# A fused residual layer on one core: loads reordered at the start, scale factors in the index row, low-rank products in fp32r parts

## The reference, cut to what matters

```
w = weights[cond]                       # (32, 64, 64), one of 200 matrices per sample
x = x + einsum('bct,bcd->bdt', x, w)    # layer 0: mixes the 64 channels
H = einsum('btd,od->bto', x, W)         # layer 1: W is 512 x 512
xa = einsum('btd,brd->btr', x, A[idx])  # rank 16, one of 8 adapters per sample
x = x + H + einsum('btr,bor->bto', xa, Bm[idx]) * scalings[idx]
```

## Time and profile before

| | |
|---|---|
| median of 3 runs | 83.15 us |
| profiled execution | 83.01 us |
| its span | 81.3 us |
| PE (matmul) busy | 74.2 us, 91% |
| DVE busy | 51.6 us, 63% |
| ACT busy | 47.6 us, 59% |
| POOL busy | 35.7 us, 44% |
| DMA | 14.58 MB, mean 179 GB/s |

### The profile page before, as it was taken

The page is one execution under the profiler, slowest core; times in us unless marked ns, Lnnn a source line. Parts: engine busy times, 40 slices in busy tenths (PEclk is TensorE's granted clock), DMA queues, the critical chain, the costliest instruction groups (busy, mean ns, idle before and its releaser), DMA issues.

```text
span 81.3 us, 1928 instructions
## 1 busy us (share of the span) xinstructions
PE 74.2 (91%) x482; PEld 67.8 (83%) x482; DVE 51.6 (63%) x125; ACT 47.6 (59%) x105; POOL 35.7 (44%) x76
## 2 busy tenths in 40 slices
PE   4999299999498999999999999999999999999950
PEld 4975288975396999999999999999999999999940
DVE  3830689150797958684868486948694878548730
ACT  0730696431988929292939394848575757375540
POOL 4200068999847653554455454465355523000000
PEclk9999999999999999999999999999999999999999
DMA  0899655589999879777897879668815452303015
GB/s 0 238 356 225 237 156 108 143 214 194 175 194 224 221 213 235 256 268 189 266 247 220 149 241 250 227 128 265 219 61 130 146 172 79 129 0 129 8 58 204
DMA packets 13198, 14.58 MB, mean 179 GB/s; under 512 B 6786, under 2 KB 8066, under 8 KB 13186
## 3 DMA queue, kind: packets, MB, share of 16 engines
q1 hardware_dynamic: 7714, 9.32, 37.5%
q0 software_dynamic: 4640, 4.23, 25.3%
q10 hardware_dynamic: 832, 0.91, 4.0%
HBM read 10.23 MB, written 4.19 MB: 177 GB/s over the span
## 4 chain that ended last, share of the span: by engine, by line
PE 65%; DMA 16%; DVE 5%; issue 5%; ACT 3%; POOL 2%; POOLq 0%; ACTq 0%
PE z_ps L566 45%; DMA scale_sb<-scales 8%; DMA b_raw<-b_t 8%; PE out_ps L601 4%; PE out_ps L619 4%; PE v_ps L595 4%; PE out_ps L615 4%; PE out_ps L614 4%; ACT w_raw L304 1%; ACT b_high L332 1%; DVE moving L438 1%; DVE b_stack L465 1%; DVE a_table L502 1%; POOL w_sb L248 1%; ACT moving L295 1%
## 5 line engine op out<-in xcount | busy, mean ns | idle before, releaser
L566 PE MATMUL z_ps<-moving,x_high 128*128 128x272 f32 x224 | 33.4, 290 | 0.0
L566 PEld LDWEIGHTS z_ps<-moving,x_high 128*128 128x128 f32 x224 | 30.8, 188 | 1.2
L240 POOL DMA_DIRECT2D b_raw<-b_t x32 | 19.6, 615 | 13.7 <-DMA w_raw<-w_t 8.1
L566 PE MATMUL z_ps<-moving,x_low 128*128 128x272 f32 x112 | 18.6, 288 | 0.0
L316 ACT ACTIVATE z_high<-z_ps 128x240 fp32r<-128x240 f32 (+1 forms) x28 | 10.7, 384 | 11.6 <-DVE low_rank L478 11.4
L233 POOL CAST moving<-a_table 128x128 fp32r x28 | 8.7, 340 | 17.4 <-PE z_ps L566 16.8
L456 DVE TENSOR_TENSOR z_low<-z_ps,z_high 128x240 fp32r<-128x240 f32 (+1 forms) x28 | 11.8, 422 | 6.9 <-ACT z_high L316 6.9
L566 PEld LDWEIGHTS z_ps<-moving,x_low 128*128 128x128 f32 x112 | 15.9, 189 | 0.0
L465 DVE TENSOR_TENSOR b_stack<-b_raw,b_high 128x512 fp32r<-128x512 f32 x16 | 11.1, 695 | 5.1 <-ACT b_high L332 4.4
L332 ACT ACTIVATE b_high<-b_raw,low_rows 128x512 fp32r<-128x512 f32 x16 | 11.5, 716 | 2.8 <-DMA b_raw<-b_t 2.8
L431 DVE TENSOR_TENSOR x_low<-x_raw,x_high 128x512 fp32r<-128x512 f32 x14 | 10.6, 754 | 0.0
(11 more groups left out here) (47 smaller groups left out, 62.6 us busy)
## 6 DMA issues: line engine op xcount, KB each, us to landing
x_raw<-xt SPq DMA_DIRECT2D x16, 256.0 KB, 5.5
b_raw<-b_t POOLq DMA_DIRECT2D x32, 128.0 KB, 4.8
out<-out_sb SPq DMA_DIRECT2D x15, 256.0 KB, 4.1
w_sb<-w SPq DMA_DIRECT2D x32, 16.0 KB, 4.0
w_raw<-w_t ACTq DMA_DIRECT2D x1, 272.0 KB, 3.4
w_raw<-w_t SPq DMA_DIRECT2D x1, 272.0 KB, 4.5
a_raw<-a_t ACTq DMA_DIRECT2D x1, 256.0 KB, 4.2
w_raw<-w_t ACTq DMA_DIRECT2D x1, 240.0 KB, 6.8
```

The costliest lines, as they stand in the source:

```text
L240: pool.dma_start(b_raw[s * C:(s + 1) * C, t % BBUFS, :], b_t[ds(which[s], 1), :, :].to_broadcast([GROUPS, RANK, OUT]),).then_inc(b_loaded[ ...
L566: last = nc.tensor.matmul(z_bank(t, part), x[:, t % XBUFS, k * P:(k + 1) * P], moving[:, int(n == HL), k, at:at + HALF], start=((n, k) == ...
```

## The change

- **First loads.** The pieces of W are reordered, so that rows 256 to 511 of the first columns come first. Both pieces of the first columns are issued on ScalarE's queue ahead of A. x of tile 0 comes in two halves, the one for rows 256 to 511 first, with a semaphore of its own. The first products go in the order k = 3, 2, 0, 1.
- **Warm-up.** 8 warm-up products become 4, then the scale product below, then 1.
- **Scale factors.** They lie behind the indices in one row (`heads`). The tensor engine spreads them over the partitions with a product of one row of ones, and VectorE copies 8 columns out. The broadcast DMA is gone.
- **Masks.** The 2048-column clearing of w0 moves from VectorE to GpSimd. The masks `low_rows` and `low_groups` become columns of `group_sb`, computed ahead of the first additions to W.
- **Low rank in parts.** For tiles 2 to 15 `take_low_rank` writes 32 columns; ScalarE spreads the high part into three groups, VectorE writes the low part into a fourth, and one fp32r product of 256 columns (by the high and low parts of `I + w` side by side) takes the place of the fp32 product of 128. `low_of_v` becomes two VectorE instructions. The high part of w0 moves from VectorE to ScalarE.
- **Order.** On the tensor engine layer 0 of tile t-1 comes before the weighing of tile t, and `plain_layer0(1)` before the weighing of tile 2. GpSimd issues `load_b` of tile 1 before `take_a` of tile 2.

```diff
-    WARM_UP = 8
+    WARM_UP = (4, 1)
+    LOW_V, LOW_B, LOW_U = 1, 2, 3
...
+    UPPER, LOWER = (0, K // 2), (K // 2, K)
+    PIECES = (((0, HALF), LOWER), ((0, HALF), UPPER), ((HALF, OUT), UPPER), ((HALF, OUT), LOWER))
+    DIAGONAL = ((2, 2 * P, HALF, 0), (0, 0, P, 1), (1, P, 2 * P, 1), (2, HALF, 3 * P, 3), (3, 3 * P, 4 * P, 3))
+    ADDED = (1, 3, 0, 5)
+    FIRST_ROWS = (K - 1, *range(K // 2, K - 1), *range(0, K // 2))
...
@@ sync
-            load_x(0)
-            load_w(1)
+            sync.dma_start(x_raw[:, 0, half:], xt[0, :, half:]).then_inc(x0_lower_loaded, 16)
+            sync.dma_start(x_raw[:, 0, 0:half], xt[0, :, 0:half]).then_inc(x_loaded[0], 16)
             load_x(1)
             load_w(3)
@@ gpsimd
-            pool.dma_start(scale_sb[:], scales.rearrange("(a n) -> a n", a=1).to_broadcast([P, ADAPTERS]),
-                           ).then_inc(scales_loaded, 16)
+            nc.gpsimd.memset(w0_sb[:], 0.0).then_inc(w0_cleared, 1)
...
             load_b(which[0], 0)
+            load_b(which[1], 1)
             pool.wait_ge(a_ready, 1)
             take_a(which[2], 2)
-            load_b(which[1], 1)
@@ scalar
             load_w(0)
+            load_w(1)
             act.dma_start(a_raw[:], a_t).then_inc(a_loaded, 16)
             load_w(2)
...
+            def high_of_w0(i):
+                first, end = BATCHES[i]
+                act.wait_ge(w0_added, i + 1)
+                nc.scalar.activation(w0_parts[:, first:end, 0, :], w0_sb[:, first:end, :],
+                                     ACT.Copy).then_inc(w0_high_ready, 1)
+            def high_of_low_rank(t):
+                act.wait_ge(low_rank_ready, t - PLAIN + 1)
+                if t >= PLAIN + 2:
+                    act.wait_ge(v_done, t - 1)
+                each = own_low_rank[:].rearrange("p s (g r) -> p s g r", g=1).to_broadcast([P, PER, LOW_U, RANK])
+                nc.scalar.activation(low_rank_parts[:, t % 2, :, 0:LOW_U, :], each, ACT.Copy).then_inc(rank_high_ready, 1)
...
                 high_of_z(t - 1, W_PART)
                 if t + 2 < TILES:
                     high_of_x(t + 2)
+                high_of_low_rank(t)
                 high_of_z(t, A_PART)
+                high_of_b(t)
                 high_of_v(t)
-                high_of_b(t)
                 take_out(t - 1)
+                if t % 2:
+                    high_of_w0(BATCH_OF[t + 1])
@@ vector
-            nc.vector.memset(w0_sb[:], 0.0).then_inc(w0_cleared, 1)
...
+            def low_of_low_rank(t):
+                dve.wait_ge(rank_high_ready, t - PLAIN + 1)
+                nc.vector.tensor_tensor(out=low_rank_parts[:, t % 2, :, LOW_U, :], in0=own_low_rank[:],
+                                        in1=low_rank_parts[:, t % 2, :, 0, :].bitcast(fp32),
+                                        op=ALU.subtract).then_inc(rank_parts_ready, 1)
...
+                if t >= PLAIN:
+                    dve.wait_ge(v_rest_ready, t - PLAIN + 1)
+                    nc.vector.scalar_tensor_tensor(out=v_stack[:, t % 2, :], in0=v_ps[t % 2][:, P:2 * P],
+                                                   scalar=group_sb[:, LOW_V:LOW_V + 1], in1=v_rest[:],
+                                                   op0=ALU.mult, op1=ALU.add).then_inc(v_ready, 1)
@@ tensor
+                    nc.tensor.matmul(v_ps[t % 2][:, 0:2 * P],
+                                     low_rank_parts[:, t % 2].rearrange("p s g r -> p (s g r)"),
+                                     w0_parts[:, t].rearrange("p h n -> p (h n)"),
+                                     start=True, stop=True).then_inc(v_done, 1)
...
+            warm_up(WARM_UP[0])
+            pe.wait_ge(index_loaded, 16)
+            nc.tensor.matmul(v_ps[0][:, 0:ADAPTERS], warm[0:1, :],
+                             index_sb[0:1, 2 * TILES * PER:2 * TILES * PER + ADAPTERS].bitcast(fp32),
+                             start=True, stop=True).then_inc(scales_done, 1)
+            warm_up(WARM_UP[1])
+            pe.wait_ge(x0_lower_loaded, 16)
+            pe.wait_ge(w_loaded[0], 16)
+            plain_products(0, W_PART, in_turn[:1])
+            pe.wait_ge(w_diag, ADDED[0])
+            plain_products(0, W_PART, in_turn[1:K // 2])
             pe.wait_ge(x_loaded[0], 16)
             pe.wait_ge(w_diag, ADDED[1])
-            plain_products(0, W_PART, range(K // 2, K)).then_inc(w_bank_done, 1)
+            plain_products(0, W_PART, in_turn[K // 2:]).then_inc(w_bank_done, 1)
...
+            plain_layer0(1)
             weigh_low_rank(2)
-            plain_layer0(1)
             w_bank(2, 2 * K, 3 * K)
...
             for t in range(3, last):
                 a_bank(t)
                 w_bank(t, 0, 2 * K)
+                whole_layer0(t - 1)
                 weigh_low_rank(t)
-                whole_layer0(t - 1)
                 w_bank(t, 2 * K, 3 * K)
```

More of the change, by code:

```diff
@@ L88, in adapted_residual_kernel @@
         w0_sb = sb("w0_sb", [P, TILES, P], fp32)
-        w0_high = sb("w0_high", [P, TILES, P], fp32r)
-        w0_low = sb("w0_low", [P, TILES, P], fp32r)
+        w0_parts = sb("w0_parts", [P, TILES, 2, P], fp32r)
         low_rank = sb("low_rank", [P, 2, PER, GROUPS, RANK], fp32)
+        own_low_rank = sb("own_low_rank", [P, PER, RANK], fp32)
+        low_rank_parts = sb("low_rank_parts", [P, 2, PER, GROUPS, RANK], fp32r)
         v_high = sb("v_high", [P, 2, P], fp32r)
+        v_rest = sb("v_rest", [P, P], fp32)
         v_stack = sb("v_stack", [P, 2, P], fp32r)
@@ L156, in read_indices @@
             _, values = nc.values_load_multi_w_load_instructions(
-                index_sb[0:1, kind, PER * t:PER * (t + tiles)], engines=(eng.engine,), min_val=0, max_val=count - 1)
+                index_sb[0:1, PER * (TILES * kind + t):PER * (TILES * kind + t + tiles)], engines=(eng.engine,), min_val=0, max_val=count - 1)
             return [values[PER * i:PER * (i + 1)] for i in range(tiles)]
@@ L332, in high_of_b @@
                 nc.scalar.activation(b_high[:, t % 2, :], b_raw[:, t % BBUFS, :], ACT.Copy,
-                                     scale=low_rows[:, 0:1]).then_inc(b_high_ready, 1)
+                                     scale=group_sb[:, LOW_B:LOW_B + 1]).then_inc(b_high_ready, 1)
             def high_of_x(t):
@@ L485, in low_of_v @@
                     dve.wait_ge(out_done, t - 1)
-                nc.vector.tensor_tensor(out=v_stack[:, t % 2, :], in0=v_ps[t % 2][:, 0:P],
-                                        in1=v_high[:, t % 2, :].bitcast(fp32),
-                                        op=ALU.subtract).then_inc(v_ready, 1)
+                dst = v_stack[:, t % 2, :] if t < PLAIN else v_rest[:]
+                nc.vector.tensor_tensor(out=dst, in0=v_ps[t % 2][:, 0:P], in1=v_high[:, t % 2, :].bitcast(fp32),
+                                        op=ALU.subtract).then_inc(v_ready if t < PLAIN else v_rest_ready, 1)
+                if t >= PLAIN:
[3 more added lines that the diff above has]
+                                                   op0=ALU.mult, op1=ALU.add).then_inc(v_ready, 1)
+            nc.vector.memset(own_rank[:], 0.0).then_inc(own_rank_ready, 1)
+            nc.vector.memset(low_rank[:], 0.0).then_inc(own_rank_ready, 1)
+            dve.wait_ge(own_rank_ready, 2)
+            for s in range(PER):
+                nc.vector.memset(own_rank[s * C:(s + 1) * C, s, :, :], 1.0).then_inc(own_rank_ready, 1)
+            dve.wait_ge(ident_ready, 1)
+            for g in (LOW_B, LOW_V):
+                rows = ident[:].rearrange("p (a g r) -> p g a r", g=GROUPS, r=RANK)[:, g, :, :]
+                nc.vector.tensor_reduce(out=group_sb[:, g:g + 1], in_=rows, axis=mybir.AxisListType.XY,
+                                        op=ALU.add).then_inc(groups_ready, 1)
+            dve.wait_ge(scales_done, 1)
+            nc.vector.tensor_copy(scale_sb[:], v_ps[0][:, 0:ADAPTERS]).then_inc(scales_ready, 1)
             add_diagonal(0)
@@ L528, in _ @@
                     low_of_x(t + 2)
+                low_of_b(t)
                 low_of_v(t)
-                low_of_b(t)
-                if t % 2 == 0:
-                    split_w0(BATCH_OF[t])
+                if t % 2:
+                    low_of_w0(BATCH_OF[t + 1])
             low_of_z(last - 1, W_PART)
             take_low_rank(last)
+            low_of_low_rank(last)
             low_of_z(last, A_PART)
@@ L551, in plain_products @@
                 at = FIRST[t % 2] + bank_of(t, part) * HALF
-                for k in ks:
+                for n, k in ks:
                     last = nc.tensor.matmul(z_bank(t, part), x_raw[:, t, k * P:(k + 1) * P],
-                                            w_raw[:, k, at:at + HALF], start=(k == 0), stop=(k == K - 1))
+                                            w_raw[:, k, at:at + HALF], start=(n == 0), stop=(n == K - 1))
                 return last
@@ L618, in layer0 @@
                     pe.wait_ge(z_low_ready[part], t - PLAIN + 1)
```

(2 more changed lines are left out.)

135 lines of the change are left out of this document (67 added, 68 removed).

## The result

The kernel before takes 83.12 us in the median of four runs, the changed one 79.77 (79.41 to 80.73, four runs). The ratio is 0.9606 with a 95% interval of 0.9522 to 0.969, so the change takes 3.3 us away; 79.9 was forecast. Without the slowest execution of each kernel (85.71 and 80.73 us, both over 1.5% above the fastest) the medians are 83.09 and 79.56. The profiled execution of the changed kernel is the longest of its four, 80.73 us with a span of 79.1. It lies 1.0 above the median, so its absolute times in the start are a little late; a second profile, of an execution of 80.29 us, has the same steady tiles.

What follows compares the result with a forecast made beforehand. The prediction took PE to bound the kernel from 26.1 us on, with waits for transfers before that. Its terms, -1.4 + 0.1 - 0.3 - 1.2 - 0.7 + 0.4 = -3.1 us, took 83.01 to 79.9, range 78.0 to 82.1.

Steps and rivals of the forecast that it cites:

- Weighing in fp32r, -1.4: Tiles 2 to 15: 14 weighing products go from 0.22 to 0.12 us each, gain 1.4 us, bounds 1.3 to 1.5.
- What it adds elsewhere: Added ScalarE and VectorE work per tile stays under PE and costs nothing; chain about 1.15 us, margin 0.6, ScalarE 84%.
- Tail, +0.1: Last tile, weighing not behind layer 0: it may wait and v is late, costing 0.1 us (0 to 0.4).
- Start, -0.3: First loads: without the broadcast A lands at 8.3, PE starts tile 1's A bank at 9.3, not 9.64; gain 0.3 us.
- b of tile 1, -1.2: PE's wait at 21.69: `load_b(1)` issued at 11.2 instead of 13.80 us removes it; gain 1.2 us, bounds 0.8 and 1.2.
- The wait at 25.60, -0.7: Weighing of tile 3: its wait of 0.39 us and its longer duration go, gain 0.7 us.
- its successor, +0.4: Before layer 0 of tile 2: a new PE wait of 0.4 us for high z, bounds 0 and 1.4.
- The clock rises later: Rival, start: fewer warm-ups delay the clock, four or five products run at half speed, at most 2.2 us, 82.1; chance 0.15.
- Everything arrives early: Rival, start: A lands near 7.4 and b of tile 2 in time; 78.6 us, down to 78.0; chance 0.17.
- The early gains are not kept: Rival, after the start: late transfers of x and b block ScalarE, leaving 1.4 and some 0.3; 81.3 us; chance 0.09.
- ScalarE as the bound: Rival, steady tiles: added copies or a missed margin make every tile 0.4 us longer than before; 85.9 us; chance 0.04.

Runs made afterwards that it cites:

- the repetition: The changed kernel run again with no edit, for a second profiled execution: 79.82 us (79.39 to 80.29), ratio 0.956 against the kernel before.

## Why the prediction held, and where it did not

*Weighing in fp32r, -1.4: right.* 0.12 us for 0.22, period 4.05, and 1.3 to 1.5 us when undone. The Trainium skill, "TensorE: Matmul & The Clock Gate" (Wait — 56ns, not 53.3ns?), would have 0.109 for 256 columns; this case's trace has 0.12, dearer by the same 10 ns as its 272 columns.

*What it adds elsewhere: right, with one reason missing.* The spread copy takes 0.285 us (0.37 allowed), the VectorE difference 0.197. Hand-overs included, the chain from the masking to the weight load takes 0.79 us, not 1.15, so the margin behind layer 0 was larger than 0.6. ScalarE is busy 7.60 us of the 10 from 30 to 40, 76% and not 84%. But an operand that comes just in time costs too, since its weights are not loaded ahead. That was not in the sum; in the changed kernel it shows in the last weighing, which takes 0.20, and probably ahead of the weighing of tile 2: PE idles 0.20 us there, until 21.50, and VectorE ends the low part of `I + w` at 21.39. *Tail, +0.1:* this 0.08.

*Start, -0.3: the size was wrong.* The step priced A by the third place of ScalarE's queue, from a row that had been measured while the broadcast slowed the loads. A landed at 6.3 (7.3 in the repetition), not 8.3. The last pieces of W gained alike. The plain products lost their pause of 1.46 us (0.16 of it is left in the repetition). A part was given back in the profiled execution: 0.45 us per plain record until about 9.7, so the bank of tile 2 starts at 14.28; it started at 15.02 in the kernel before. The whole of the scale step was worth 1.8 us, and that holds part of the waits below, which the sum booked apart.

*b of tile 1, -1.2: the wait went, the reason was wrong.* The line on its order is worth nothing. It was the earlier last piece of W, by 1.6 us and not 0.7, that let GpSimd go on. And the step took PE to wait no more before a product with v; it waits 1.21 us at 19.14, for tile 0's, and the sum has no term for that. That b had been in time in the kernel before only because PE was late: issued 1.4 us earlier it landed at 16.0, where it had landed at 15.7.

*The wait at 25.60, -0.7, and its successor, +0.4.* The first went. The second did not come: b of tile 2 landed at 19.7, not 21.7, and layer 0 of tile 2 starts without idle time ahead, at 24.71 here and at 24.18 in the repetition, where the forecast had 23.9.

The sum came out by luck, since two errors cancel: the start gained more than 0.3, and b's steps less than 1.2 + 0.7 - 0.4. Together these terms are -1.8, and the new way of the scale factors alone brought 1.8: the size is met, the causes are not those of the forecast. By the runs, of the 3.3 us 1.8 are the scale factors' way and 1.3 to 1.5 the weighing in parts behind layer 0; the order of the first loads, the order of b and the number of warm-ups are each within 0.2 of nothing.

*The rivals.* "The clock rises later" came true as an event, near 9.7 in one profile and 7.4 in the other against 7.3 in the kernel before, but not as a price: seven warm-ups bring it to 6.8 and the time stays. It had been priced as though PE were the bound there, and the landing of b was. "Everything arrives early" describes the loads, not the time, for the same reason. "The early gains are not kept" falls with the constant rest in the table. ScalarE as the bound is refuted by PE, which is busy all of the 10 us from 30 to 40.

## What to carry over

Before a landing is priced by its place in a queue, look at the rate of the DMA around it: where it dips while transfers are outstanding, a small transfer in scattered pieces may be slowing all others, and the row's price goes when that transfer goes. A wait that is removed early in a kernel pays only up to the next late arrival; find that one by taking each transfer's landing and counting the copies queued behind it. A cheaper instruction whose operand has a longer way pays only if other work stands between.
